# ScalarE's side work three scan states later in a two-layer state-space and expert kernel

## The reference

```python
x = x + scan0(ctx, layernorm(x))          # z = layernorm(x) is the gate
x = x + moe0(layernorm(x))                # top-1 of 8 experts + shared expert
x = x + scan1(ctx, layernorm(x))
x = x + moe1(layernorm(x))                # top-2 of 8 experts + shared expert

# scan, for each of 512 channels, with 16 states n:
dA = exp(delta_t * A[n]);  h[n] = h[n] * dA + (delta_t * u_t) * B_t[n]
y_t = sum_n h[n] * C_t[n] + D * u_t;      out_t = y_t * silu(z_t)

# shared expert and routed expert e
h = silu(x @ gate) * (x @ up);            out = h @ down
```

## Time and profile before

| | us |
|---|---|
| median of 3 runs | 2397.37 |
| lowest and highest | 2394.19, 2400.5 |
| the profiled execution: its time | 2404.08 |
| its span, first to last instruction | 2402.1 |
| mean granted clock of TensorE, share of 2.4 GHz | 0.903 |
| busy: TensorE, VectorE, GpSimd, ScalarE | 1959.0, 1415.0, 989.3, 855.9 |

### The profile page before, as it was taken

One profiled execution on the slowest core, in us unless ns is written; L12 is line 12 of the kernel. 1 busy time (PEld: TensorE's weight loads), 2 busy tenths in 40 slices (PEclk: granted clock), 3 DMA queues, 4 the chain that ended last, 5 costly groups with the idle time before them and its releaser, 6 DMA issues. The chain is left out here.

```text
span 2402.1 us, 18775 instructions
## 1 busy us (share of the span) xinstructions
PE 1959.0 (82%) x5107; PEld 901.3 (38%) x5107; DVE 1415.0 (59%) x1962; ACT 855.9 (36%) x1392; POOL 989.3 (41%) x889
## 2 busy tenths in 40 slices
PE   8837678788787795599999973889599999999990
PEld 2212233233233341144444432445255555555540
DVE  6869988888887878797888844654010111111113
ACT  5545545364544444555656420110011111111110
POOL 0057766666575665887777731211400000000005
PEclk9968889899898997799999985999799999999995
DMA  5044354302203004368687645211654555455536
GB/s 185 22 194 105 140 110 107 112 5 99 89 8 153 1 14 155 138 225 339 224 305 277 215 153 189 68 50 58 242 179 152 180 180 166 160 179 180 175 123 214
DMA packets 100992, 352.50 MB, mean 147 GB/s; under 512 B 15200, under 2 KB 15200, under 8 KB 82464
## 3 DMA queue, kind: packets, MB, share of 16 engines
q1 hardware_dynamic: 93216, 326.21, 39.7%
q0 software_dynamic: 7680, 25.17, 3.1%
HBM read 288.29 MB, written 63.05 MB: 146 GB/s over the span
## 5 line engine op out<-in xcount | busy, mean ns | idle before, releaser
L561 POOL TENSOR_TENSOR work<-work,big 128x512 f32<-128x512 f32 x512 | 658.5, 1291 | 265.7 <-DVE bank L608 263.9
L474 PE MATMUL bank<-work,ident 128*128 128x512 f32 x928 | 536.9, 693 | 226.5 <-DVE work L592 175.9
L608 DVE TENSOR_TENSOR_SCAN bank<-bank,work 128x512 f32<-128x512 f32 x512 | 624.9, 1221 | 137.5 <-ACT bank L528 88.9
L528 ACT ACTIVATE bank<-work,An 128x512 f32<-128x512 f32 x512 | 345.9, 691 | 256.2 <-DVE work L592 253.1
L474 PEld LDWEIGHTS bank<-work,ident 128*128 128x128 f32 x928 | 179.5, 216 | 521.6 <-DVE work L592 333.7
L592 DVE TENSOR_TENSOR work<-bank,big 128x512 f32<-128x512 f32 x512 | 343.9, 672 | 9.1 <-PE bank L474 8.8
L1655 POOL DMA_INDIRECT W<-ys_d,slot x32 | 33.9, 1059 | 644.4 <-PEq L1642 634.9
L1612 PE MATMUL bank<-Y,big 128*128 128x512 f32 x528 | 263.6, 596 | 0.0
L1195 DVE SCALAR_TENSOR_TENSOR work<-work,bank 128x352 f32<-128x352 f32 (+1 forms) x63 | 36.6, 581 | 329.0 <-ACT work L1185 328.9
L957 PE MATMUL bank<-W,work 128*128 128x512 f32 x384 | 198.6, 622 | 0.0
L1173 ACT COPY work<-bank 128x512 f32<-128x512 f32 x63 | 36.9, 585 | 396.9 <-PE bank L1158 396.9
(11 more groups left out here) (249 smaller groups left out, 2252.8 us busy)
## 6 DMA issues: line engine op xcount, KB each, us to landing
big<-bc_d SPq DMA_DIRECT2D x64, 1024.0 KB, 6.7
work<-gate SPq DMA_DIRECT2D x39, 704.0 KB, 4.2
work<-up SPq DMA_DIRECT2D x39, 704.0 KB, 4.1
W<-gate SPq DMA_DIRECT2D x24, 1024.0 KB, 4.9
W<-up SPq DMA_DIRECT2D x24, 1024.0 KB, 5.5
W<-down SPq DMA_DIRECT2D x24, 1024.0 KB, 5.4
work<-down SPq DMA_DIRECT2D x39, 512.0 KB, 3.8
work<-xs_d SPq DMA_DIRECT2D x63, 256.0 KB, 4.4
```

The costliest lines, as they stand in the source:

```text
L474: nc.tensor.matmul(YS[:, :], ident[:, :], hC[ring(g * NS + u[0])], start=v == 0, stop=v == len(units[g]) - 1).then_inc(sum_done, 1)
L528: nc.scalar.activation(H[i % 4][:, :], delta[g % 2], ACT.Exp, scale=An[vb // B][:, g % NJ, i:i + 1]).then_inc(dA_done, 1)
L561: nc.gpsimd.tensor_tensor(dBu[i % 2], du[g % 2], Bb[:, i, :], ALU.mult).then_inc(dBu_done, 1)
L608: nc.vector.tensor_tensor_scan(H[i % 4][:, :], H[i % 4][:, :], dBu[i % 2], 0.0, ALU.mult, ALU.add).then_inc(scan_done, 1)
```

## The change

ScalarE's loop no longer calls `side.step` for state s behind exp(s), but for state s-3. The last three calls come behind the loop. The pieces of `gate` are called on their own and stay where they were. All other engines keep their order, and no wait, buffer or instruction is added or removed. Behind L530 the lines of the changed kernel have numbers higher by 5 (L1023 becomes L1028, L1038 becomes L1043, L1185 becomes L1190, and so on).

```diff
                     if y_at[g] + 3 <= i <= y_at[g] + 5 and g < GROUPS - 1:
                         prep(g + 1, i - y_at[g] - 3)
-                    side.step("act", act, vb, n)
+                    if vb <= B:
+                        side.gate("act", act, vb, *divmod(n, NS))
+                    if s >= side.LAG:
+                        side.step("act", act, *divmod(s - side.LAG, NJ * NS))
+                for s in range(GROUPS * NS - side.LAG, GROUPS * NS):
+                    side.step("act", act, *divmod(s, NJ * NS))
                 side.after("act", act)
...
             def step(self, name, eng, b, n):
                 last = isinstance(b, int) and b == B
-                if not last or n < NS:
+                if name != "act":
                     self.gate(name, eng, b, *divmod(n, NS))
...
             def gate(self, name, eng, b, j, i):
-                first = isinstance(b, int) and b == 0
-                if first and j == 0:
+                first = b == 0
+                if first and j == 0 or b == B and j:
                     return
...
-            PAIRS = 5 * NJ
+            PAIRS, LAG = 5 * NJ, 3
```

## The result

| | before | after |
|---|---|---|
| median of four runs each, us | 2398.09 | 2421.04 |
| lowest and highest | 2394.19, 2400.5 | 2418.56, 2425.51 |
| the profiled execution: time, span | 2404.08, 2402.1 | 2418.56, 2416.3 |
| mean granted clock | 0.903 | 0.901 |

The ratio is 1.0099, with a 95% interval of 1.0079 to 1.012: slower by about 23 us. The two profiled executions are 14.2 us apart in span, because that of before was the slowest of its kernel's runs and that of after the fastest of its own. Forecast were 2414 us and a range of 2392 to 2430.

A forecast was written before the change was run, and what follows sets the result against it. VectorE's chain was taken to bound batches 1 to 4 and TensorE the routed experts; gains of 36.1 us against losses of 53.0 gave net +16.9, so 2414 us on the median, range 2392 to 2430.

The forecast's parts named there:

- gain 1: Ends of batches 1 to 3: copies of states 59 and 63 no longer hold back exponentials; 26 us gained.
- the tanh of state 54: Batches 1 to 3: it waits for a 256 KB write and comes at most 0.5 us earlier; 1.5 us gained for three.
- gain 2: End of batch 4: the same two copies no longer keep scans 4.27 and 4.92 us; 8.6 us gained.
- loss 1: State 22, batches 1 to 3: the tanh of state 21 falls behind the long preparation, VectorE waits; 5.7 us lost.
- loss 2: State 34, batches 1 to 3: late bank-freeing copy stops TensorE's down product 3.9 us, then it runs slow; 15.6 us lost.
- loss 3: Batch 4: late tanh at state 20 (4.4 us), late copy before TensorE's up product at state 34 (4.3); 8.7 us lost.
- loss 4: Batch 5, scatter of the rows: ScalarE's row falls behind the long preparation and GpSimd waits; 3.0 us lost.
- loss 5: Routed experts: tanh and copies behind nine long preparations stop TensorE; 33 us less 13 of earlier stops, net 20 lost.
- Rival A: Losses in the expert stretch are covered, TensorE catches up within the next tile; 2394 us, break-even, chance 0.2.
- Rivals B and C: B: faster, losses 1 to 3 half as large, 2370 or 2385 us, 0.12. C: no effect, 2397, counted with rival A.
- D: Worse: each stop runs into the next preparation; 2432 us and more, chance 0.06.
- The drain of a table load: Skill's 1.38 us per switch, left out; would delay pieces behind the long preparation, some 14 us more over ten.

The follow-up runs named there:

- kernel 3: Against the kernel before: ScalarE's pieces three states later only from state 54 in batches 1 to 3 and from state 40 in batch 4; 2365.39 us, ratio 0.9857.
- kernel 1: Against the kernel before: ScalarE's pieces three states later only up to batch 4, scatter and routed experts as before; 2395.35 us, ratio 0.9979.
- kernel 2: Against the kernel before: only the routed experts' pieces of ScalarE (from batch 5, state 25) three states later; 2421.29 us, ratio 1.0092.
- kernel 4: Against the kernel before: only the routed experts' pieces moved, as in kernel 2, but none past a preparation step; 2401.77 us, ratio 1.001.
- kernel 9: Kernel 3 with the lag from state 58 instead of 54, and SyncE's writes of the shared expert's output one frame place earlier; 2358.43 us, ratio 0.9823.
- kernels 11 and 12: First: the changed kernel with a lag of one instead of three, 2358.54 us. Second: kernel 9 plus a lag of one for all other ScalarE pieces, 2346.2 us.
- kernel 10: Against the kernel before: only the routed experts' copies three states later, their tanh kept, no copy past a preparation step; 2434.79 us, ratio 1.0156.

## Why the prediction was right, term by term

The forecast (slower, 2414) held, and so did its shape: what gains, what loses and where. The change is 23 us by the medians where 17 were forecast. The terms against the scan starts of the two profiles:

| term | forecast | found | where |
|---|---|---|---|
| gain 1, with the tanh of state 54 | -27.5 | -29.5 | 54 to 7, three ends |
| gain 2 | -8.6 | -7.5 | 4:44 to 4:52 |
| loss 1 | 5.7 | 5.4 | state 22, three times 1.8 |
| loss 2 | 15.6 | 14.4 | 23 to 54, three times |
| loss 3 | 8.7 | 5.3 | 4:20 to 4:44 |
| loss 4 | 3.0 | 2.7 | 5:1 to 5:8 |
| loss 5 | 20 | 25.4 | 5:22 to 7:63 |
| sum | 16.9 | 16.3 | 16.8 at 7:63 |

That the two sums agree to 0.6 us is in part luck: the profile of before was 6 us above its median, and a term can be off by a few us in one pair of profiles. The runs by themselves, each with an interval of 3 to 6 us either way, say: gains 34 (kernel 3; forecast 36.1), losses 1 to 3 together 29 (kernel 3 against kernel 1; 30.0), loss 5 22 (kernel 2; 20). With loss 4 that makes 20 of the 23; the rest belongs to no term.

*Gain 1* was right in mechanism, and kernel 3 shows that it is kept to the end. Of it the tanh of state 54 was mis-sized: forecast were 1.5 us for three, and the scans behind it come 1.1, 1.0 and 1.3 earlier. The wait at state 4 of the next batch did go; that for an exponential at state 7 grew from 0.34 to 0.61.

*Loss 2* was right in total with one part of it mis-sized. The stop was forecast at 3.9 us and is 3.71. The slow stretch was taken as 3.6 us of half speed and lasts some 9 us, from 366.4 to 375, at a granted clock of 0.50, the level of 1.2 GHz. VectorE's wait is 7.00, not 5.2. In the profile of after this was partly hidden in batches 1 and 2, since VectorE came to state 34 3.0 us earlier than before, for a reason that has nothing to do with the change (below); the jump of the scans is 7.1, 7.1 and 5.8 us. Undone, the loss is 15.6 us by the scan starts and 14 by the ratios. Besides there is a stop that the prediction did not have: in state 54 of these batches TensorE waits 3.35 us for the copy of the hidden tile, which stands behind the long preparation. The scans behind it do not show it: VectorE waits there for the tanh in any case.

*Loss 3* was too large, 8.7 against 5.3. State 20 came as forecast (5.4, less 1.2 behind it). In state 34 the scans jump by 5.8 us, not 4.3, and in another way: TensorE stands still for 2.96 (3.1 forecast) and then is not slow at all, but VectorE waits 2.51 us for the sum and behind it 3.04 for a tanh that had to pass the long preparation.

```profile
854.36 1.13 PE L962 MATMUL bank<-W,work 128*128 128x512 f32 x2 [2.96 <-ACT work L1038]
```

```profile
847.00:890.00 43.00, 39.03 (x111) 18.04 (x109) 35.22 (x45) 21.76 (x33) 26.58 (x24) 1.00 0.04 14
```

And before there had been a copy in state 40 that held a scan for 2.62 us, and its going gave 3.9 back. That step was not in the sum, although the rows of the same engine show it.

*Loss 5*, named the least certain, was 5 too small by the scan starts, and 2 both by kernel 2's ratio and by the scan starts against kernel 1, which has the old order there (22.3). The count of idle time of TensorE was right, 29 us against "25 to 35". The first preparation has 6.9 us (5:34 to 5:40) against 6.5, but this is luck, for its parts are others. TensorE's rows:

```profile
1031.78 1.98 PE L1152 MATMUL bank<-W,work 128*128 128x512 f32 x4 [1.83 <-ACT work L1183]
...
1039.71 3.67 PE L1163 MATMUL bank<-W,work 128*128 128x512 f32 x8 [1.65 <-issue]
1043.94 0.33 PE L1135 MATMUL bank<-ident,work 128*128 128x128 f32 x1 [0.56 <-DVE work L1205]
```

The stop ahead of the up product is right (1.83 against 2.0). That for VectorE's second step was put at 2.8 and is 0.56. Between them is one of 1.65 ahead of the down product that the prediction did not have, shown as "issue": its bank has to be freed by ScalarE's copy of x, which came behind the tanh and ended at 1039.61. And TensorE did not run slow here (granted clock 1.00 from 1030 to 1054). The working by kinds does not come out either: where the tanh stands behind the long step the scans jump by 7.7, 7.6 and 8.2 us at one state (6.5, 4.7 and 6.5 forecast), and over the 16 states around the third, sixth and seventh preparation, those of the copies, they lose 0.4, 0.4 and 1.7, net of the stops of before that went (3.1, 2.1 and 2.9 forecast, not net). Moved alone, each kind makes a loss of another sort. That VectorE's wait for the tanh is covered away from the preparations is shown by kernel 4.

*Rival A* fell with kernel 2. In the prediction stood the rule of the Trainium skill (Perfetto Trace Analysis, Identifying the Most-Contended Engine) by which a TensorE with 45% of weight loading would not be the bound. The traces do not agree: TensorE was busy 364.73 of 376 us before, 18 us more idle time made the stretch 24 us longer, and with a lag of one 7 us less made it 10 shorter.

*Rivals B and C* fell with the changed kernel itself: the waits of losses 1 and 2 came at nearly their full size, and the gap of 5.43 us is gone. D, 2432 us and more, did not come.

*The drain of a table load* of the Trainium skill (ScalarE: Activation LUTs, What ACT_TABLE_LOAD costs) did not show: in kernel 9 a load begins at 408.52, when the activation ahead ends (407.80 and 0.71), and the tanh follows at 409.82, 1.30 us behind.

What I did not see was how little of the lag the gains need. The prediction looked at three states only as given; the rule that it found itself, "the lag removes its lead over the consumers", says that one state would cost a third of the lead, and kernels 11 and 12 are 41 and 51 us faster than the kernel before.

## What to carry to other kernels

When an engine that feeds two others blocks on a late input, moving that piece behind the next independent work pays where the input is late and can cost where it was early, so move it by place and by the smallest distance that frees the consumer. Before moving, look what long step stands in the way and which bank or buffer the piece frees. And move pieces of one chain together: to leave one of them in place turns the order round.

## What the runs showed of the chip

**The granted clock differs between executions of the same order.** Up to the routed experts (5:25) the kernel before and kernel 10 have the same instructions in the same order. TensorE in state 32 of batch 1, before and then kernel 10:

```profile
351.75 1.13 PE L474 MATMUL bank<-work,ident 128*128 128x512 f32 x2 [1.10 <-DVE work L592]
354.28 2.08 PE L474 MATMUL bank<-work,ident 128*128 128x512 f32 x2 [1.41 <-DVE work L592]
```

```profile
350.42 1.12 PE L474 MATMUL bank<-work,ident 128*128 128x512 f32 x2 [1.10 <-DVE work L603]
352.95 1.12 PE L474 MATMUL bank<-work,ident 128*128 128x512 f32 x2 [1.41 <-DVE work L603]
```

The idle times ahead are the same, 1.10 and 1.41 us, and behind them the pair takes 2.08 in one and 1.12 in the other. The windows agree:

```profile
353.50:357.00 3.50, 2.72 (x3) 1.18 (x4) 3.50 (x6) 0.69 (x1) 2.65 (x3) 0.52 0.97 212
```

```profile
353.50:357.00 3.50, 3.50 (x13) 1.78 (x12) 2.83 (x4) 1.71 (x4) 2.60 (x3) 1.00 0.98 215
```

VectorE's wait for the sum just behind was 3.83 us before and 0.80 in kernel 10. At the same state kernel 10 gains another 3.0 us in batch 2 and 1.4 in batch 3, and by 5:22 it was 12.5 us ahead of the kernel before with no difference in the order. How much of the rest is the clock's stays open. The Trainium skill, TensorE: Matmul & The Clock Gate, Part 1, says of the start of a kernel that the number of slow matmuls varies between runs of it. These rows are not of the start; they show the like in the middle, with 3 us at a single place.

**A stop can cost more than itself.** Behind 3.71 us of idleness in batch 1 TensorE ran at half speed for 9 us, and VectorE waited 7.00. But behind the 2.96 us in batch 4 (854.36) it went on at a granted clock of 1.00, so the price of a stop is not fixed.
